# A graph network's edge counting on one Trainium2 core: two numbers per partition in each comparison, and loads signalled apart

## The reference, cut to what matters

```python
h = relu(layernorm(x)); x = x + L0(h)   # 10 rounds of a weighted segment_sum over the edges
h = relu(layernorm(x)); x = x + L1(h)   # three graph convolutions, in-degrees with self loops
h = relu(layernorm(x)); x = x + L2(h)   # relu(h[src] + edge_attr_96), segment_sum, two matmuls
h = relu(layernorm(x)); x = x + L3(h)   # gated messages, segment_sum, update, layernorm
```

## Time and profile before

| what | us |
|---|---|
| median of 3 runs | 3220.68 |
| lowest and highest run | 3216.37, 3226.22 |
| span of the profiled execution | 3215.5 |
| start of the table building on DVE | 18.86 |
| first comparison of the counting loop | 51.86 |
| end of the loop (start of `normalize_relu`) | 615.16 |
| last instruction of the stage (L383) | 633.55 |
| DVE busy from 52 to 616 | 455.32 of 564 |

### The profile page before, as it was taken

One profiled execution on the slowest core, in us unless ns is written; L12 is line 12 of the kernel. 1 busy time (PEld: TensorE's weight loads), 2 busy tenths in 40 slices (PEclk: granted clock), 3 DMA queues, 4 the chain that ended last, 5 costly groups with the idle time before them and its releaser, 6 DMA issues.

```text
span 3215.5 us, 74018 instructions
## 1 busy us (share of the span) xinstructions
PE 2704.0 (84%) x25686; PEld 2215.9 (69%) x25687; DVE 2379.8 (74%) x6312; ACT 760.0 (24%) x1393; POOL 1204.5 (37%) x1205
## 2 busy tenths in 40 slices
PE   3676777899999998887999999998599888888984
PEld 0211121499999998887999999897477666767763
DVE  6988777763233347457988888887699999999986
ACT  0123455440000004010211111111133333323321
POOL 0000000000000000000777777775377777777771
PEclk9999999889999999898999999999699999999996
DMA  1000000000000000001544444442234333343330
GB/s 30 0 0 0 0 0 0 1 3 2 2 2 2 1 2 3 3 1 26 142 121 118 119 117 118 116 121 55 76 107 107 106 106 103 105 107 101 106 99 21
DMA packets 108158, 180.84 MB, mean 56 GB/s; under 512 B 36346, under 2 KB 69900, under 8 KB 107867
## 3 DMA queue, kind: packets, MB, share of 16 engines
q0 software_dynamic: 47824, 89.19, 11.6%
q1 hardware_dynamic: 60043, 87.59, 9.6%
HBM read 171.88 MB, written 4.80 MB: 55 GB/s over the span
## 4 chain that ended last, share of the span: by engine, by line
POOL 34%; issue 11%; DVE 5%; PE 2%; DMA 1%; ACT 0%; DVEq 0%; POOLq 0%; ACTq 0%
POOL gate_rows L1346 20%; POOL msg_rows L975 13%; DVE pre_space L1049 2%; PE msg_sums L1171 1%; DMA first_rows<-pre_space 0%; DVE msg_rows L1073 0%; DVE pre_space L1469 0%; PE gate_sums L1600 0%; DMA msg_rows<-h_rows,all_src_i 0%; PE msg_sums L1186 0%; ACT msg_src_near L987 0%; DMA msg_src_row<-src_rows 0%; DVE pre_space L1141 0%; DVE msg_rows L1069 0%; DVE pre_space L1534 0%
## 5 line engine op out<-in xcount | busy, mean ns | idle before, releaser
L1346 POOL DMA_INDIRECT gate_rows<-first_rows,all_src_i x637 | 648.5, 1018 | 198.9 <-issue 193.8
L975 POOL DMA_INDIRECT msg_rows<-h_rows,all_src_i x539 | 534.1, 991 | 164.1 <-issue 163.5
L962 POOL MEMSET pre_middle<- 125x1 f32 x1 | 0.1, 98 | 1515.6 <-POOLq L651 1515.6
L1171 PE MATMUL msg_sums<-pre_parts,pre_space 125*128 125x192 f16 x6125 | 524.7, 247 | 39.4 <-DVE pre_space L1049 39.3
L1171 PEld LDWEIGHTS msg_sums<-pre_parts,pre_space 125*128 125x128 f16 x6125 | 506.7, 98 | 45.9 <-DVE pre_space L1049 41.4
L581 PE MATMUL hop_sums<-dense_work,dense_counts 125*128 125x192 f16 x6250 | 522.0, 247 | 15.5 <-DVE dense_work L541 8.2
L581 PEld LDWEIGHTS hop_sums<-dense_work,dense_counts 125*128 125x128 f16 x6250 | 519.3, 98 | 18.0 <-DVE dense_work L541 6.2
L1575 PE MATMUL gate_sums<-pre_space,pre_parts 125*96 125x384 f16 x2450 | 457.8, 348 | 5.4 <-DVE pre_parts L1443 5.4
L424 PE MATMUL cnt_sums<-cnt_hot,cnt_near 128*128 x1000 | 347.7, 408 | 119.5 <-DVE cnt_hot L363 114.3
L1575 PEld LDWEIGHTS gate_sums<-pre_space,pre_parts 125*96 125x96 f16 x2450 | 314.5, 132 | 138.2 <-issue 29.6
L1049 DVE TENSOR_SCALAR pre_space<-msg_src_near,pre_node_no 125x640 f16<-125x640 f16 x1225 | 393.5, 394 | 11.7 <-ACT msg_src_near L987 11.6
(11 more groups left out here) (272 smaller groups left out, 3289.1 us busy)
## 6 DMA issues: line engine op xcount, KB each, us to landing
msg_edge<-edges SPq DMA_DIRECT2D x98, 384.0 KB
msg_src_row<-src_rows SPq DMA_DIRECT2D x49, 312.5 KB
gate_edge<-edges SPq DMA_DIRECT2D x98, 128.0 KB
gate_rows<-first_rows,all_src_i POOLq DMA_INDIRECT x637
gate_src_row<-on_src SPq DMA_DIRECT2D x49, 187.5 KB
msg_rows<-h_rows,all_src_i POOLq DMA_INDIRECT x539
gate_inputs<-on_edges SPq DMA_DIRECT2D x49, 48.0 KB, 1.9
first_rows<-pre_space SPq DMA_DIRECT2D x6, 375.0 KB
```

The lines of the kernel that those rows point to most:

```text
L975: nc.gpsimd.indirect_dma_start(out=rows[:, r, k, :], out_offset=None, in_=table, in_offset=bass.IndirectOffsetOnAxis(ap=src_i[:, at:at + 1 ...
L1171: last = nc.tensor.matmul(got[group % 2][:, n, 0:2 * D], pick[:, c % 2, j, i * EP:(i + 1) * EP], parts[:, j, :], start=(j == 0), stop=(j = ...
L1346: nc.gpsimd.indirect_dma_start(out=rows[:, r, k, :], out_offset=None, in_=table, in_offset=bass.IndirectOffsetOnAxis(ap=src_i[:, at:at + 1 ...
```

## The change

A comparison no longer takes the code of the window. It takes the edge's `key` and a second number per partition, `start_at` of the window, which holds `-500 * w`: `(iota - key) == -500 * w` is the same question. So `own`, `shift_keys`, `shifted` and `begun` go, and with them the wait at the start of each window. The window's entry of `start_at` is addressed by the window's number, which is `i * 12 + j` with `i` in a register. The four loads get three semaphores: DVE starts on `dst_groups` alone, waits for POOL's constants after three instructions, for `src` and `dst` before L299, and for `x` only ahead of `normalize_relu`. SP issues the load of `x` only when `dst_groups` has arrived.

```diff
--- before.py
+++ after.py
@@ -141,7 +141,6 @@
         key = m.sb("key", [EP, ET + 2], F32)
         src_n = m.sb("src_n", [EP, ET + 2], F16)
         start_at = m.sb("start_at", [EP, NW + 2], F32)
-        own = work[:, 2 * NT * D:2 * NT * D + 4 * (ET + 2)].bitcast(F32).rearrange("p (a c) -> p a c", a=2)
         wins = work[0:1, 0:2 * (NW // WG + 1) * WROW].bitcast(I32)
         ones = m.sb("ones", [NP, 1], F16)
 
@@ -173,12 +172,13 @@
         table_ps = tables_ps[:, 0, :]
         wins_ps = tables_ps[:, 1, :]
         steps_ps = tables_ps[:, 2, :]
-        loaded = m.sem("loaded"); made = m.sem("made"); chain = m.sem("chain")
+        groups_loaded = m.sem("groups_loaded"); ends_loaded = m.sem("ends_loaded"); x_loaded = m.sem("x_loaded")
+        made = m.sem("made"); chain = m.sem("chain")
         root_asked = m.sem("root_asked"); root_done = m.sem("root_done")
         parts = m.sem("parts"); turned = m.sem("turned"); spans = m.sem("spans"); rows = m.sem("rows")
         tables = m.sem("tables"); placed = m.sem("placed"); degrees = m.sem("degrees")
         ready = [m.sem(f"ready{i}") for i in range(2)]
-        used = m.sem("used"); shifted = m.sem("shifted"); begun = m.sem("begun")
+        used = m.sem("used")
         emptied = [m.sem(f"emptied{b}") for b in range(WB)]
         ident = g["ident"]
         part_w = [(0, 128), (128, NW - 128)]
@@ -199,10 +199,11 @@
 
         @block.sync
         def _(sp):
-            sp.dma_start(groups_i, dst_groups).then_inc(loaded, 16)
-            sp.dma_start(src_i, src).then_inc(loaded, 16)
-            sp.dma_start(dst_i, dst).then_inc(loaded, 16)
-            sp.dma_start(g["x"][:, :, :], x.rearrange("(t p) d -> p t d", p=NP)).then_inc(loaded, 16)
+            sp.dma_start(groups_i, dst_groups).then_inc(groups_loaded, 16)
+            sp.dma_start(src_i, src).then_inc(ends_loaded, 16)
+            sp.dma_start(dst_i, dst).then_inc(ends_loaded, 16)
+            sp.wait_ge(groups_loaded, 16)
+            sp.dma_start(g["x"][:, :, :], x.rearrange("(t p) d -> p t d", p=NP)).then_inc(x_loaded, 16)
 
         @block.gpsimd
         def _(pool):
@@ -237,25 +238,17 @@
         @block.scalar
         def _(act):
 
-            def shift_keys(w, j):
-                nc.scalar.activation(own[:, j % 2, :], key[:, :], ACT.Identity,
-                                     bias=start_at[:, bass.ds(w, 1)]).then_inc(shifted, 1)
-
-            def empty(w, b, wide, end, j=None):
+            def empty(w, b, wide, end):
                 act.wait_ge(used, end + 2)
-                if j is not None:
-                    shift_keys(w + 2, j)
                 to = g["counts"][0:NP, :].rearrange("p (h w) -> p h w", w=CW)[:, :, bass.ds(w * WIN, wide)]
                 got = sums[0:NP, b, 0:WIN * NT].rearrange("p (t h) -> p h t", h=NT)[:, :, 0:wide]
                 nc.scalar.activation(to, got, ACT.Copy).then_inc(emptied[b], 1)
 
             act.wait_ge(tables, 1)
-            for j in range(2):
-                shift_keys(j, j)
             with act.Fori(0, NW // WG) as i:
                 bounds, _ = windows(mybir.EngineType.Activation, i)
                 for j in range(WG):
-                    empty(i * WG + j, j % WB, WIN, bounds[j + 1], j)
+                    empty(i * WG + j, j % WB, WIN, bounds[j + 1])
             bounds, _ = windows(mybir.EngineType.Activation, NW // WG, NW % WG)
             for j in range(NW % WG):
                 w = NW - NW % WG + j
@@ -266,14 +259,14 @@
         @block.vector
         def _(dve):
             link = Chain(dve, chain)
-            dve.wait_ge(loaded, 64)
-            dve.wait_ge(made, 11)
+            dve.wait_ge(groups_loaded, 16)
             link(nc.vector.tensor_copy(groups_f, groups_i))
             by_tile = groups_f.rearrange("p (c e) -> p c e", c=GT)
             link(nc.vector.tensor_reduce(tmin, by_tile, AX, ALU.min))
             link(nc.vector.tensor_reduce(tmax, by_tile, AX, ALU.max))
 
             wide = [NG, NW, GT]
+            dve.wait_ge(made, 11)
             mins = tmin.unsqueeze(1).to_broadcast(wide)
             maxs = tmax.unsqueeze(1).to_broadcast(wide)
             link(nc.vector.tensor_tensor(in_lo, mins, spread(last, GT), ALU.is_le))
@@ -296,6 +289,7 @@
             link(nc.vector.tensor_scalar(strides, strides, ROUND, -ROUND, ALU.add, ALU.add))
             link(nc.vector.tensor_scalar(strides, strides, 1.0, None, ALU.add))
 
+            dve.wait_ge(ends_loaded, 32)
             link(nc.vector.tensor_copy(src_f, src_i))
             link(nc.vector.tensor_scalar(high, src_f, 1.0 / NP, -(NP // 2) / NP, ALU.mult, ALU.add))
             link(nc.vector.tensor_scalar(high, high, ROUND, -ROUND, ALU.add, ALU.add))
@@ -347,36 +341,34 @@
             dve.reg_mov(at, 0)
             dve.reg_mov(turn, 1)
 
-            def compare(w, j, begin, end, lo):
-                nth = dve.snap(w + 1)
+            def compare(w, begin, end, lo):
+                origin = start_at[:, bass.ds(w, 1)]
                 dve.reg_mov(tile, lo)
                 dve.reg_mov(upto, end)
-                dve.wait_ge(shifted, nth)
-                dve.sem_inc(begun, 1)
                 with dve.Fori(begin, upto):
                     dve.wait_ge(used, turn)
                     slot, hots, nears = slot_parts(dve, at)
                     now = within(nc, dve.snap(tile), ET - 1)
                     low = src_n[:, bass.ds(now, 2)].unsqueeze(1).to_broadcast([EP, 128, 2])
                     nc.vector.tensor_tensor(nears.rearrange("p (c i) -> p c i", i=2), pairs2, low, ALU.is_equal)
-                    codes = own[:, j % 2, :]
-                    nc.vector.tensor_scalar(hots[0], iota, codes[:, 0:ET][:, bass.ds(now, 1)], None,
-                                            ALU.is_equal).then_inc(ready[0], 1)
-                    code = codes[:, 1:ET + 1][:, bass.ds(now, 1)]
+                    nc.vector.tensor_scalar(hots[0], iota, key[:, 0:ET][:, bass.ds(now, 1)], origin,
+                                            ALU.subtract, ALU.is_equal).then_inc(ready[0], 1)
+                    code = key[:, 1:ET + 1][:, bass.ds(now, 1)]
                     dve.reg_add(turn, turn, 1)
                     dve.reg_mov(tile, now + 2)
                     dve.reg_mov(at, slot * -1 + BANK)
-                    nc.vector.tensor_scalar(hots[1], iota, code, None, ALU.is_equal).then_inc(ready[1], 1)
+                    nc.vector.tensor_scalar(hots[1], iota, code, origin,
+                                            ALU.subtract, ALU.is_equal).then_inc(ready[1], 1)
 
             with dve.Fori(0, NW // WG) as i:
                 bounds, lows = windows(mybir.EngineType.DVE, i, lows=True)
                 for j in range(WG):
-                    compare(i * WG + j, j, bounds[j], bounds[j + 1], lows[j])
+                    compare(i * WG + j, bounds[j], bounds[j + 1], lows[j])
             bounds, lows = windows(mybir.EngineType.DVE, NW // WG, NW % WG, lows=True)
             for j in range(NW % WG):
-                compare(NW - NW % WG + j, j, bounds[j], bounds[j + 1], lows[j])
-            dve.wait_ge(shifted, NW // WG * WG + 2)
-
+                compare(NW - NW % WG + j, bounds[j], bounds[j + 1], lows[j])
+
+            dve.wait_ge(x_loaded, 16)
             normalize_relu(nc, link, root_asked, root_done, dve, g["x"][:, :, :], g["h"][:, :, :],
                            g["work32"][0:NP, NT * D:2 * NT * D].rearrange("p (t d) -> p t d", d=D), g["s"], 1)
             dve.wait_ge(degrees, 1)
```

## The result

| | before | after |
|---|---|---|
| median of 13 runs each, us | 3224.94 | 3235.95 |
| lowest and highest | 3216.37, 3232.09 | 3234.20, 3243.74 |
| span of the profiled execution | 3215.5 | 3233.9 |
| first L361 (after: L353) | 51.86 | 38.54 |
| loop: from there to L101 | 563.3 | 588.65 |

The changed kernel is slower, 11.0 us by the medians: ratio 1.0037, 95% interval 1.0030 to 1.0044. The forecast of 3236.0 is the measured 3235.95, partly by luck: it was built on a median of 3220.7 from three runs, and with ten more that median is 3224.9. The size to judge is the difference, +15.6 forecast and +11.0 measured; in the stage itself it is +12.0.

What follows compares the result with a forecast made beforehand. The prediction took DVE's own sequencer to bound the loop. Its terms, -14.4 (loads) - 20 (window changes) + 50 (second number) = +15.6 us, on 3220.7 gave 3236; range 3193 to 3262.

Steps and rivals of the forecast that it cites:

- What bounds the kernel: Counting loop: DVE's own sequencer, not its data path, ACT or PE, sets the 0.96 us between pairs.
- Loads: -14.4: Stage start: DVE, released by `dst_groups` alone, starts at 4.5 instead of 18.86 us; -14.4 us, bounds 11.6 and 15.0.
- The floor of 13.0: Stage start: gain in us kept even if DVE stood still until POOL's constants are over at 5.82.
- Window change: -20: Start of each window: two or three sequencer steps go, 0.13 us at 156 window changes; -20 us, bounds -16 and -24.
- The excess: Extra time of a window change over a pair in the loop: 0.31 us before, forecast to fall to 0.18.
- ACT's shifts: 0: Loop: 150 us of ACT work leave, all beside DVE, so no gain; bounds 0 and -1 us.
- Second number, sequencer: +50: Ahead of L363: three more address operations cost 0.10 us in each of 500 pairs; +50 us, bounds 25 and 78.
- The lower end: Least price of a packed sequencer operation in a pair: 0.10/6 = 0.017 us each, 0.05 for three.
- Second number, data path: free: L363 and L369: second operation and second read fit within the pair; 0.91 us needed, still under 0.94.
- Steps hidden or formed once per window: Rival, 17%: the pair's added address operations cost nothing, leaving -14.4 - 20 = -34.4 us: 3186.
- The cheap end: Rival, 15%: only 0.06 to 0.08 us more per pair, cancelled by the two gains; -5 to +6, about 3219.
- The lost fast form: Rival, 6%: two numbers per partition slow each comparison's data path, by 0.13 or 0.39 us; 3254 to 3496.

## Why the prediction was right, and where it was not

*What bounds the kernel.* Right. The sequencer sets the pace: two steps that feed nothing cost 0.084 us per pair, and a pair took as long with comparisons of 407 ns at a fixed address (0.970) as with 345 (0.967).

*Loads: -14.4.* 13.3 at the first comparison (38.54), inside the bounds of 11.6 and 15.0. The start was nearly met (4.23 for 4.5). What was missed is POOL: while its last constant runs, the cast doesn't finish. The floor of 13.0, for a DVE that stands still until POOL is through, was nearly the truth. 37.5 was 1 us early.

*Window change: -20.* -26, and -2 at the group changes, which lies outside the bounds of -16 and -24. The excess fell to 0.133, forecast 0.18, taken as two to three steps of 0.052. In the compiled program four instructions are left of six, so it was two, the wait and a move, which took 0.18 us together: an average over unlike steps is not the price of those that go.

*ACT's shifts: 0.* Right: 150 us of ACT gone, and the loop is what the distances on DVE make it.

*Second number, sequencer: +50.* +47 (0.094 times 500). The size is right, but one of its ends was wrongly derived. The lower end read the distances L361 to L363 (0.21) and L363 to L369 (0.31) as both set by the sequencer, six steps apart. The unused steps show that the first is set by the data path. For the same reason the excess was looked for in the wrong place: L354 starts 0.24 behind L353, not 0.31, and the rest comes between L354 and L360 (0.38 instead of 0.31). And no even price per step holds. Ahead of L354 the compiled program has six operations in one packed instruction, which is then full, and one addition by itself; before there were four. The packs take 57 ns with three operations (fixed address), 69 with four and 93 with six, that is 12 ns for each of these operations, below the forecast's least price of 17. An operation by itself takes 40 to 45 ns and some 30 to the next instruction. Where the window's number in its group is 0 the addition is missing, and a pair with the short L353 costs 0.028 more; in the other windows it costs 0.10 to 0.11, so the lone addition takes about 0.08. The unused steps fit this (0.084 for one more instruction). The mask does not follow from these prices alone (0.039 and 0.045), since the operations that it replaced were worth more than 12 ns each. The +50 was the middle between 0.017 and 0.052 a step, and the truth was two steps below the one end and one beyond the other: the sum came out by luck.

*A place in the code: not forecast.* +6 from the 24 slow pairs of window 8. The prediction has no term for it. It nearly makes up for the window changes, which gave 8 more than forecast.

*Second number, data path: free.* Wrong in size, without effect here. "Last about as long as before" was 407 ns for 345. The needed distance is 0.32 and not the 0.28 that the later stages' rows gave, so a pair with the long L353 needs 0.98 us, more than the 0.94 that it had; not "still under". It was covered only because the sequencer had grown slower still. Where the address is fixed it binds.

*The rivals.* Steps hidden or formed once per window: fell with the unused steps; its 3186 is near what the fixed address gave (3183.3), as it should be. The rule of the Trainium skill cited with it ("Advanced Engine Details and Errata", Sequencer Loop) has instructions queued while the sequencer goes on; the delay that comes out one instruction late fits that. But in this loop the sequencer doesn't get far enough ahead to hide a step. The cheap end: fell in the loop (0.094 per pair), though the measured +11.0 lies nearly as near to its +6 as to the forecast's +15.6. (Its -5 to +6 on 3220.7 make 3216 to 3227, so its middle is 3221 and not 3219.) The lost fast form: fell, 0.06 us from start to start where it wanted at least 0.13.

*The sum.* -13.3 - 26 - 2 + 47 + 6 = +12 in the stage (12.0 read), for +15.6.

## What to carry to other kernels

Where instructions with register operands follow each other closely, as three in 0.96 us here, compare the distance between starts in two pairs whose durations differ. If it is the same, count sequencer instructions and not engine time: the view by source line lists them with their durations. Keep loop variables out of operand addresses, with an immediate per unrolled step and a rare update of the data. Compare the distances window by window too, since the same code can cost more at one place of an unrolled loop, and that price moves with every instruction added or taken. Test this with steps whose result nobody uses before trading register work for data-path or ACT work. A distance between two starts belongs to the data path or to the sequencer, each for itself; only the period tells which one sums up.

## What was not expected of the hardware

- A second number per partition lengthens a comparison of 128x500 f16 from 345 to 407 ns and its least distance from start to start from 0.26 to 0.32 us, while a second operation with an immediate leaves 345 and 348 ns.
- Register work of a pair is never hidden in this loop: 12 ns for each operation more in the packed instruction ahead of the first comparison (57, 69 and 93 ns), some 0.08 us for an instruction more (0.084 for one of 53 ns). A mask in place of a multiplication in the register work made each pair 0.039 us slower (0.045 in a second kernel).
- At one place of the unrolled code a pair of the changed kernel takes 1.30 us and more instead of 1.06 to 1.08. In six of the ten kernels such pairs fill window 7 or 8 of each group, 0.24 us dearer than the others; in the other four a window change there takes 0.12 us more.
- A cast of 98x1024 int32 to f32 took 2.15 us beside POOL's last constants and 0.69 after them. It ended 0.55 us after the last of them.
